# Null-key attention: weighted sums one step later, one bank for projections, both maxima ahead of the copies

## The reference, cut to what matters

```
h  = layernorm(x)
q  = split_heads(h @ Wq) * 64 ** -0.5
k, v = split_heads(context @ Wkv)
k  = concat(null_kv[0], k)       # a 257th, learned key and value in every head
v  = concat(null_kv[1], v)
attn = softmax(q @ k.T)
x  = x + layernorm_scaled((attn @ v) @ Wout)
```

## Time and profile before

| | |
|---|---|
| runs | 1118.01, 1119.61, 1120.69 us; median 1119.61 us |
| profiled execution, its own time | 1116.3 us |
| its span | 1114.5 us |
| null-key attention, steps 0 to 31 and the end | about 876.6 to 1041.3 us of the span |
| busy over the span | TensorE 88%, VectorE 74%, ScalarE 57%, GpSimd 38% |

### The profile page before, as it was taken

The page is one execution under the profiler, slowest core; times in us unless marked ns, Lnnn a source line. Parts: engine busy times, 40 slices in busy tenths (PEclk is TensorE's granted clock), DMA queues, the critical chain, the costliest instruction groups (busy, mean ns, idle before and its releaser), DMA issues.

```text
span 1114.5 us, 18229 instructions
## 1 busy us (share of the span) xinstructions
PE 979.7 (88%) x5958; PEld 720.5 (65%) x5958; DVE 823.2 (74%) x1980; ACT 636.2 (57%) x1594; POOL 426.2 (38%) x664
## 2 busy tenths in 40 slices
PE   5688999999759998868999999996899999998587
PEld 4457887888513434746777777775667777777465
DVE  7855898898667881698989988768665667675663
ACT  3373666766317775366797877973144666664121
POOL 8231122111121110235766767767130565654200
PEclk9697999999859998899999999997899999999789
DMA  5530211122052310300000000303000100003000
GB/s 215 139 122 1 76 39 39 39 67 62 20 170 81 98 40 20 152 1 1 1 1 1 1 1 1 151 1 121 1 1 21 57 1 2 1 14 138 1 1 20
DMA packets 32254, 53.55 MB, mean 48 GB/s; under 512 B 4192, under 2 KB 24448, under 8 KB 31008
## 3 DMA queue, kind: packets, MB, share of 16 engines
q1 hardware_dynamic: 29616, 50.03, 13.5%
q10 hardware_dynamic: 2544, 2.36, 0.7%
HBM read 45.33 MB, written 6.88 MB: 47 GB/s over the span
## 4 chain that ended last, share of the span: by engine, by line
PE 64%; DVE 16%; ACT 9%; issue 6%; DMA 2%; POOL 1%; SPq 1%; DVEq 0%; ACTq 0%
PE psum L1733 8%; PE psum L1356 8%; PE psum L1366 7%; ACT region_d L1795 4%; PE psum L2524 3%; PE psum L1763 3%; PE psum L2453 3%; PE psum L412 3%; PE psum L368 2%; DVE region_d L1931 2%; ACT region_c L1812 2%; PE psum L1719 2%; PE psum L2427 2%; PE psum L2469 2%; DVE null_work L2626 2%
## 5 line engine op out<-in xcount | busy, mean ns | idle before, releaser
L1733 PE MATMUL psum<-gated_parts 128*128 128x512 f32 x768 | 191.1, 400 | 18.7 <-DVE region_d L1931 15.1
L1733 PEld LDWEIGHTS psum<-gated_parts 128*128 128x128 f32 x768 | 137.0, 188 | 69.1 <-DVE region_d L1931 36.8
L2024 POOL TENSOR_TENSOR region_d<-region_d 128x256 f32<-128x256 f32 x126 | 94.6, 751 | 93.1 <-DVE region_d L1931 91.0
L1425 ACT ACTIVATE rounds_work<-psum,region_c 128x512 f32<-128x512 f32 x128 | 84.6, 688 | 28.1 <-PE psum L1356 25.9
L802 DVE TENSOR_REDUCE work<-psum 128x1 f32<-128x512 f32 x128 | 81.8, 686 | 22.0 <-PE psum L368 20.3
L1356 PE MATMUL psum<-parts,split 128*128 128x512 f32 x384 | 95.9, 400 | 0.0
L1366 PE MATMUL psum<-parts,split 128*128 128x512 f32 x384 | 93.3, 392 | 0.0
L1547 POOL CAST parts<-rounds_work 128x1024 fp32r<-128x1024 f32 x32 | 33.4, 1043 | 151.9 <-ACT rounds_work L1425 151.9
L1795 ACT ACTIVATE region_d<-psum,gated_work 128x128 f32<-128x128 f32 x256 | 75.9, 447 | 26.8 <-issue 22.2
L1479 DVE TENSOR_TENSOR parts<-rounds_work,parts 128x1024 fp32r<-128x1024 f32 x64 | 76.3, 1220 | 16.9 <-POOL parts L1547 15.9
L1795 ACT ACTIVATE region_d<-psum,ctx 128x128 f32<-128x128 f32 x256 | 73.0, 375 | 25.2 <-PE psum L1733 15.4
(11 more groups left out here) (450 smaller groups left out, 2190.6 us busy)
## 6 DMA issues: line engine op xcount, KB each, us to landing
rounds_work<-cw_rows SPq DMA_DIRECT2D x32, 256.0 KB, 3.4
region_a<-in_l1v SPq DMA_DIRECT2D x8, 512.0 KB, 4.0
region_b_last<-in_l1o SPq DMA_DIRECT2D x1, 4096.0 KB, 12.3
region_a<-in_l2f SPq DMA_DIRECT2D x1, 4096.0 KB, 12.0
region_b_last<-in_l3f_small SPq DMA_DIRECT2D x1, 4096.0 KB, 12.8
region_a<-in_l3f SPq DMA_DIRECT2D x1, 2080.0 KB, 7.4
region_c<-in_l0f SPq DMA_DIRECT2D x1, 2076.0 KB, 12.3
region_c<-in_l3x SPq DMA_DIRECT2D x1, 2048.0 KB, 7.8
```

The costliest lines, as they stand in the source:

```text
L1425: act.activation(H[g % 2][:, f, :], bank[f], ACT.Gelu_apprx_tanh, bias=W("b1")[:, (g % E) * FT + f:(g % E) * FT + f + 1]).then_inc(h_ready ...
L1733: ins = pe.matmul(bank[2 * (n % 2) + c], src[a][:, t * P:(t + 1) * P], weights[b][:, piece(c)], start=m == 0, stop=m == len(PASSES) - 1)
L2024: pool.tensor_tensor(tile[:, 0:2, :], tile[:, 0:2, :], tile[:, 2:4, :], ALU.add).then_inc(k.pool_chain, 1)
```

## The change

- The weighted sums of step n stand in step n + 1, after its scores and its first projection. They have bank 7 (the last two: banks 2 and 3). `turn` no longer waits for `av_sb`.
- From projection 8 on, all projections use bank 6. Projection n waits for projection n - 1.
- VectorE takes both maxima before the copies; ScalarE copies the first projection between the two exponentials.
- The first projection of a step stands before the turns on TensorE, the second behind them.
- Step 30 (p = 7, b = 2) makes no outputs; step 31 makes those of both batches.

```diff
     def bank_of(n):
-        return k.bank[1 + n] if n < 2 else k.bank[6 + n % 2]
+        return k.bank[1 + n] if n < 2 else k.bank[6 + n % 2] if n < FIRST else k.bank[6]
+
+    def sums_at(n):
+        return k.bank[n - STEPS + 4][:, 0:S] if n >= STEPS - 2 else k.bank[7][:, 0:S]
...
             if n >= 4:
-                pe.wait_ge(proj_sb, n - 1)
-                if n >= 6 and MADE[n - 2][0] != "v":
-                    pe.wait_ge(*proj_low.at(LOWS[n - 2]))
+                same = n - 1 if n > FIRST else n - 2
+                pe.wait_ge(proj_sb, same + 1)
+                if n >= 6 and MADE[same][0] != "v":
+                    pe.wait_ge(*proj_low.at(LOWS[same]))
...
             if g >= 2:
-                if g % 2 == 0:
-                    pe.wait_ge(av_sb, g // 2)
-                else:
-                    pe.wait_ge(pt_sb, g - 1)
+                pe.wait_ge(pt_sb, g - 1)
...
+        def weighted_sums(n):
+
+            p, b = divmod(n, B)
+            pe.wait_ge(pt_sb, 2 * n + 2)
+            pe.wait_ge(proj_sb, made("v", p // 2, b))
+            if n == 0:
+                pe.wait_ge(proj_sb, FIRST)
+            else:
+                pe.wait_ge(av_sb, n)
...
+        for n in range(STEPS):
+            p, b = divmod(n, B)
+            if n + 1 < STEPS:
+                scores(*divmod(n + 1, B))
+            for m in MADE_IN[p][b][:1]:
+                project(m)
+            if n > 0:
+                weighted_sums(n - 1)
+            for i in range(2):
+                turn(2 * n + i)
+            for m in MADE_IN[p][b][1:]:
+                project(m)
+            if p + 1 == PAIRS and b != 2:
+                h = b // 2
+                pe.wait_ge(*cleared.at(h + 1))
+                pe.wait_ge(av_sb, B * (PAIRS - 2) + b + 1)
+                for t in range(TPB * b, TPB * (b + 1)) if h == 0 else range(4, 8):
+                    output(t, range(PAIRS - 1))
+        turn_null_weights(0)
+        weighted_sums(STEPS - 1)
...
+        for n in range(STEPS):
+            p, b = divmod(n, B)
+            if n + 1 < STEPS:
+                exponentials(2 * n + 2)
+            for m in MADE_IN[p][b][:1]:
+                projections(m)
+            if n + 1 < STEPS:
+                exponentials(2 * n + 3)
+            if n > 0:
+                take_sums(n - 1)
+            for m in MADE_IN[p][b][1:]:
+                projections(m)
...
             if more:
                 maxima(g + 2)
+                maxima(g + 3)
+                reciprocals(g + 2)
+            for n in here[:1]:
+                if MADE[n][0] != "v":
+                    low_projections(n)
             copy_turned(g)
             if more:
-                maxima(g + 3)
-                reciprocals(g + 2)
+                reciprocals(g + 3)
             copy_turned(g + 1)
-            if more:
-                reciprocals(g + 3)
-            p, b = divmod(g // 2, B)
-            if b < 2:
-                for n in MADE_IN[p][b]:
+            for n in here[1:]:
+                if MADE[n][0] != "v":
                     low_projections(n)
```

More of the change, by code:

```diff
@@ L2502, in tensor @@
             project(n)
-        pe.wait_ge(nvw_sb, 1)
[L2504 to L2510, removed]
-                for n in MADE_IN[p][b]:
[L2512 to L2527, removed]
@@ new lines, in weighted_sums @@
+        def weighted_sums(n):
[6 more added lines that the diff above has]
+                pe.wait_ge(av_sb, n)
+            for kt in range(TPB):
+                for j in range(2):
+                    ins = pe.matmul(sums_at(n)[j * DH:(j + 1) * DH, :], V[p // 2 % 2][:, b * TPB + kt, p % 2 * P + j * DH:p % 2 * P + (j + 1) * DH],
+                                    PT[(2 * n + j) % 4][:, kt, :], start=kt == 0, stop=kt == TPB - 1,
+                                    tile_position=(0, j * DH))
+            ins.then_inc(av_psum, 1)
@@ L2563, in projections, with clear_output, take_sums @@
             ins.then_inc(proj_sb, 1)
[L2565 to L2572, removed]
+        def clear_output(h):
+            if h == 0:
+                act.wait_ge(proj_sb, len(MADE))
+                act.wait_ge(*proj_low.at(LOWS[-1]))
+            else:
+                act.wait_ge(av_sb, STEPS - 2)
+            act.activation(bank[6 + h].rearrange("p (a n) -> p a n", n=P),
+                           k.ident[:, :].unsqueeze(1).broadcast_to([P, HALF // P, P]), ACT.Copy, scale=0.0)\
+                .then_inc(cleared.semaphore, 1)
+        def take_sums(n):
+            p, b = divmod(n, B)
+            act.wait_ge(av_psum, n + 1)
+            act.activation(oT[p][:, b * S:(b + 1) * S], sums_at(n), ACT.Copy).then_inc(av_sb, 1)
         def take_null_weights(h):
@@ L2590, in scalar @@
         projections(BEHIND_X + 2)
[L2591 to L2604, removed]
+        for n in range(STEPS):
+            p, b = divmod(n, B)
+            if n + 1 < STEPS:
[8 more added lines that the diff above has]
+                projections(m)
+            if n == STEPS - B - 1:
+                clear_output(0)
+            if n == STEPS - 2:
+                clear_output(1)
+        take_null_weights(0)
+        take_sums(STEPS - 1)
         take_null_weights(1)
@@ L2658, in vector @@
             more = g + 2 < ITEMS * PAIRS
+            here = MADE_IN[g // 2 // B][g // 2 % B]
             if more:
                 maxima(g + 2)
+                maxima(g + 3)
[3 more added lines that the diff above has]
+                    low_projections(n)
             copy_turned(g)
             if more:
-                maxima(g + 3)
-                reciprocals(g + 2)
+                reciprocals(g + 3)
             copy_turned(g + 1)
-            if more:
-                reciprocals(g + 3)
-            p, b = divmod(g // 2, B)
-            if b < 2:
-                for n in MADE_IN[p][b]:
+            for n in here[1:]:
+                if MADE[n][0] != "v":
                     low_projections(n)
```

1 line of the change is left out of this document (added).

## The result

| | before | changed |
|---|---|---|
| median of the runs made together | 1118.81 us (4) | 1140.87 us (4; 1129.66 to 1143.82) |
| ratio, 95% interval | 1 | 1.0166 (1.0119 to 1.0213) |
| the same again, two more groups of 4 | 1 | 1.0169 (1.0108 to 1.0230), 1.0154 (1.0095 to 1.0213) |
| profiled execution, its span | 1116.3, 1114.5 us | 1129.7, 1127.9 us |
| first to last scores of the attention | 152.73 us | 165.39 us |

The changed kernel is slower by 1.5 to 1.7% (intervals 1.0 to 2.3%). In the profiled executions the attention accounts for +12.66 and its end for +1.99, together +14.65 us. By steps (distances from one start of the scores to the next) the four steps b = 0 to 3 of a pair went from 5.04, 5.04, 4.64, 4.64 to 5.67, 5.99, 5.21, 4.58.

The account below looks back on a forecast made before the run. Projecting steps were taken as bound by TensorE's own work, the others by the ring. Six pairs +11.8, pair 6 0, steps 28 and 29 0, end +2.0: +13.8 us, 1133.4 us; range 1124 to 1139.

Parts of the forecast that it names:

- Part 1: Sums one step later, maxima first: pair 6, b = 2 and 3, fall from 4.64 to 4.1 and 3.8 us, -1.4 in all.
- the ring: Scores, maximum, exponentials, reciprocal, copy, sums, next scores: 4.64 us without projections, TensorE waiting 1.62; costs q/k steps nothing.
- Part 2: One projection bank: handover of q 2.36 us, k 3.06, delaying b = 0 to 2; +1.97 us per four steps, +11.8 for six pairs.
- the 0.04 from an end to a waiting engine: Delay from one engine's end to a waiting engine's start, 0.04 us, used in the handovers of q and k.
- Part 3: A fourth change of TensorE's tiling in steps that project: 0.15 us taken, range 0 to 0.3; b = 0 said not to depend on it.
- Part 4: Last pair and end: steps 28 and 29 unchanged; step 30's scores to step 31's sums 13.24 us for 11.27, +2.0.
- Rival A: Bank handover hidden in the 14 q/k steps, no tiling price, the cut ring pays: -1.9 to -2.9 us, about 1117.2; chance 0.06.
- B: Handover hidden, but the fourth tiling change costs 0.15 us in each of 26 projecting steps: +1.5, 1121.1; chance 0.05.
- C: Delays on VectorE and ScalarE feed each other, 0.3 us in q/k steps and v steps behind them: +6, 1139; chance 0.12.
- the walk: Four steps of a pair followed engine by engine, giving about 5.5, 5.95, 5.3, 4.6 us for 5.05, 5.05, 4.64, 4.64.
- D: TensorE's clock falls in the new holes of 0.3 to 0.7 us, one q/k step per pair: +35 us, 1168; chance 0.02.

Follow-up runs that it names:

- e5: Changed kernel with q/k low parts from projection 8 on made as zeros by a one-operand operation from SBUF, freeing the bank after ScalarE's copy: 1126.1 us, ratio 1.0051.
- e9: Changed kernel with q's copy ahead of both exponentials on ScalarE and q's low part ahead of the even item's reciprocal on VectorE: 1127.9 us, ratio 1.0073.
- e4: Kernel before, all orders kept, with projections from 8 on in bank 6 alone, each waiting for the one before: 1179.2 us in its one execution.
- e12: Changed kernel with the odd item's maximum put back behind the copy of the even turned item on VectorE: 1174.0 us in its one execution.
- e2: Changed kernel with low parts of q and k made from two SBUF operands, freeing the bank after ScalarE's copy: 1135.3 us, ratio 1.0156.
- e11: Kernel before with late sums in steps 26 and 27 only, step 30's in bank 2, both maxima first there, bank 6 cleared earlier: ratio 0.9977.
- e7: Kernel before with late sums in steps 26 and 27 only and step 30's sums in bank 2, maxima's order unchanged: ratio 1.0067.

## Why the prediction was right

Forecast: +13.8 us, 1133.4 us, range 1124 to 1139, slower with 0.89. Measured: slower; +14.65 us by the traces; by the ratio 1.0166 on the 1119.6 us that the forecast started from, 1138.2 us, near the upper end. The raw median of 1140.9 lies 1.9 above it. The mean clocks of those four executions (0.935 to 0.925) put them at 147 to 171 us at the lower level, where the kernel before has 154 in the mean, which at 0.35 us for each is more than these 1.9; in which layer it stood, only the profiled one of the four shows. The repeats gave 1136.0 and 1134.4.

- *Part 1* holds: 4.14 and 3.70 for pair 6, b = 2 and 3, against 4.1 and 3.8; TensorE's waits for the ring are gone.
- *Part 2* holds to a few hundredths: k at 4.11 (4.04 forecast), q at 1.58 (1.58), k at 4.45 (4.47), v at 1.58 (1.58). The steps were 5.67, 5.99, 5.21, 4.58 for 5.52, 5.95, 5.27, 4.61: +2.09 for four steps where +1.97 was forecast. e5 shows the bank as the cause, e9 that b = 0 is ScalarE's and VectorE's order, e4 that only the new orders keep the single bank cheap. One link was too short: the 0.04 from an end to a waiting engine was read where ScalarE waits for VectorE, and from the low part's end to TensorE it is 0.15.
- *Part 3* took 0.15 for every step; it is 0.20 in a q/k step (b = 0 of e5 and e9) and 0.12 in a v step (b = 3). That the four steps came out within 0.12 of the forecast is in part luck: b = 0 and 1 were 0.15 and 0.04 too short in it, b = 2 and 3 0.06 and 0.03 too long. The sentence that b = 0 does not depend on this price was wrong: a part of it falls behind k, from whose start to the next scores it is 1.55, not 1.48. That, and k at 4.11, is nearly all of b = 0's missing 0.15.
- *Part 4*: 13.26 forecast as 13.24, sums of step 30 at 4.53 as 4.54.
- *Rival A* (handover hidden) and *B* fall by the low parts' 10.3 us. *C* falls: from pair to pair a step varies by no more than 0.03, and each stands within 0.15 of the walk. *D* falls for this change, whose holes of up to 0.7 us in each step (1.3 in the first) left the clock at 1.00; but e4 shows its mechanism, at 2.6 us.
- Not seen in the prediction: how much the order of the maxima matters. It was booked as part of cutting the ring; e12 shows that late sums without it would have cost some 40 us more (A 207.9 for 165.4).

## What to carry to other kernels

A PSUM bank in a ring of engines is priced by its handover, from the first matmul into it to the last reader's end (here 2.4 and 3.1 us), against the work that stands between its two uses; add it up from one place in the trace where it went unhindered, then check in each engine's fixed order what stands ahead of each link. Before freeing one resource to cut a wait, look at the steps where that wait is zero: here the 14 q/k steps had none and became 0.6 to 0.95 us longer each, and six v steps behind them 0.57, while the ring gave back 1.4 us in two steps. And when an operation moves later, everything queued behind its consumer moves too, so two edits that look separable (late sums, maxima first) may be worth nothing or a disaster alone.

## What the runs showed of the hardware that was not expected

- **VectorE waits for GpSimd once its operand leaves PSUM.** With one operand in PSUM and one in SBUF the 128 x 512 operation takes 0.69 us, GpSimd's 1.04 us operation beside it or not. With both in SBUF it takes 0.69 alone (L1473) and 1.49 or 1.29 when GpSimd is at work (e2), ending 0.54 after it. The Trainium skill (SBUF — State Buffer, Who interferes with whom) says that VectorE and GpSimd share a pair of SBUF ports, that an instruction with two SBUF inputs or a fast single-input one needs it, and that whichever comes second blocks fully. The traces agree, with the ends 0.54 and 0.28 behind GpSimd's. GpSimd, which came first in the rows shown, kept its 1.04. The other order is in e2 too: GpSimd's cast of weights (L2742), which begins 0.6 before the end of k's low part in b = 1, takes 0.75 us in each of its six times, where the kernel before has 0.29 for it. Here, moving an operand out of PSUM to free a bank bought a wait of up to 0.8 us on VectorE.
- **Which holes the clock bore.** Granted 1.00 is the upper level, 2.4 GHz; a mean below it holds time at the lower one, 1.2 GHz. Holes of 1.51 and 1.62 us left it at 1.00; so did one of 2.11 followed by one of 0.68 (e11). Two of 2.10 and 2.00 in a row (e7) were followed by the lower level:

```profile
1009.70:1018.80 9.10, 5.04 (x50) 3.78 (x48) 6.12 (x13) 4.48 (x18) 3.68 (x7) 1.00 1.01 406
1018.80:1029.00 10.20, 7.38 (x41) 5.79 (x42) 2.97 (x7) 3.60 (x12) 3.83 (x7) 0.70 0.12 51
```

But the length of the holes alone does not decide it. In e12 holes of 2.09 and 2.00 stand ahead of and behind each step b = 3 of six pairs, with the same groups of TensorE around them; four of these steps kept 1.00 and two fell to 0.80 and 0.79 right behind the first hole. A pair that fell and the next one:

```profile
893.00:912.00 19.00, 13.56 (x98) 10.20 (x98) 9.27 (x20) 7.50 (x26) 7.10 (x12) 0.91 0.01 1
912.00:931.00 19.00, 13.78 (x107) 10.05 (x107) 8.62 (x19) 8.82 (x31) 9.27 (x16) 1.00 0.00 1
```

In e4, too, 3 of the 14 holes of 2.60 left the clock at 1.00. What decides between equal holes stays open. The Trainium skill (TensorE: Matmul & The Clock Gate, A second HAM failure mode: psum-queue depth-cycling) describes a clock that goes up and down with short idle times between groups. These traces agree for some holes of 2 us and more, and not for those of up to 0.7 in each step.
